# Token mixer's convolution: one PSUM bank for the turned spectra, two for the product back to time

## The reference

```python
logits = (x @ Wl.T + bl).reshape(Bq, Tq, H, K)          # K = 31 taps, H = 4 heads
w = softmax(where(valid, logits, -inf), axis=-1)
xg = x.reshape(Bq, Tq, H, d)[:, clip(pos, 0, Tq - 1)]
y = einsum('bthk,btkhd->bthd', w, xg).reshape(Bq, Tq, Cq)
y = y.transpose(0, 2, 1) + bias[None, :, None]
z = conv_general_dilated(y, Wc, (1,), 'VALID')           # Wc: 512 x 128 x 31
z = selu((z + bc[None, :, None]).transpose(0, 2, 1))
return z @ W2.T + b2                                     # 512 -> 128
```

## Time and profile before

| | before |
|---|---|
| median of 3 runs (lowest, highest) | 2428.52 us (2428.08, 2430.85) |
| profiled execution, its own time | 2426.93 us |
| its span | 2425.1 us |
| PE busy | 2096.5 us (86%) |
| DVE busy | 1616.2 us (67%) |
| ACT busy | 1200.1 us (49%) |
| POOL busy | 914.1 us (38%) |
| mean granted clock of TensorE | 0.932 |

### The profile page before, as it was taken

The page is one execution under the profiler, slowest core; times in us unless marked ns, Lnnn a source line. Parts: engine busy times, 40 slices in busy tenths (PEclk is TensorE's granted clock), DMA queues, the critical chain, the costliest instruction groups (busy, mean ns, idle before and its releaser), DMA issues. The chain is left out here.

```text
span 2425.1 us, 43279 instructions
## 1 busy us (share of the span) xinstructions
PE 2096.5 (86%) x14951; PEld 1497.0 (62%) x14951; DVE 1616.2 (67%) x3612; ACT 1200.1 (49%) x2015; POOL 914.1 (38%) x763
## 2 busy tenths in 40 slices
PE   6789999969997799999999997999999995687761
PEld 5568887835553566666666665777777773555540
DVE  5333456447775888888888874766766765666663
ACT  2333344335552567666767674655656552332330
POOL 0000000014443577777778781000000001876772
PEclk9899999979998799999999999999999996668995
DMA  7670000049900100000000000000000001214554
GB/s 271 228 259 26 26 28 10 1 189 419 396 5 1 70 1 1 0 0 0 0 0 0 0 1 20 1 0 0 0 0 0 0 1 46 89 42 129 169 144 156
DMA packets 64710, 165.38 MB, mean 68 GB/s; under 512 B 12450, under 2 KB 43476, under 8 KB 55100
## 3 DMA queue, kind: packets, MB, share of 16 engines
q1 hardware_dynamic: 51580, 148.24, 17.1%
q0 software_dynamic: 7104, 12.71, 1.5%
q10 hardware_dynamic: 5888, 2.62, 0.4%
HBM read 68.62 MB, written 96.86 MB: 68 GB/s over the span
## 5 line engine op out<-in xcount | busy, mean ns | idle before, releaser
L1279 POOL TENSOR_TENSOR c_both<-c_hid 128x512 f32<-128x512 f32 x384 | 492.0, 1289 | 142.4 <-ACT c_hid L1252 104.8
L1252 ACT ACTIVATE c_hid<-c_scaled,c_b 128x1024 f32<-128x1024 f32 x384 | 437.0, 1150 | 171.1 <-DVE c_scaled L1326 156.2
L1326 DVE TENSOR_TENSOR c_scaled<-c_p_h,c_shares 128x1024 f32<-128x1024 f32 x384 | 454.6, 1215 | 79.2 <-PE c_p_h L1195 77.9
L1200 PE MATMUL c_p_o<-c_both,c_w 128*128 128x512 f32 x768 | 390.7, 591 | 0.0
L1193 PE MATMUL c_p_h<-c_x_hi,c_w_hi 128*128 128x512 f32 x384 | 290.8, 757 | 2.6 <-DVE c_w_lo L1349 2.6
L642 POOL TENSOR_TENSOR d_ln_rstd<-d_ln_var,d_ln_power 128x2 f32<-128x2 f32 x48 | 33.5, 697 | 526.1 <-DVE d_ln_var L638 526.1
L1200 PEld LDWEIGHTS c_p_o<-c_both,c_w 128*128 128x128 f32 x768 | 144.4, 188 | 35.5 <-issue 2.2
L247 POOL COPY a_work<-a_vec 128x64 f32<-128x64 f32 x4 | 1.2, 303 | 409.1 <-PE a_p_A L338 223.6
L1510 PEld LDWEIGHTS d_p_s<-d_kk,d_q_bd 128*128 128x128 f32 x768 | 123.9, 192 | 45.9 <-issue 45.9
L1195 PE MATMUL c_p_h<-c_x_hi,c_w_lo 128*128 128x512 f32 x384 | 152.0, 396 | 0.0
L1194 PE MATMUL c_p_h<-c_x_lo,c_w_hi 128*128 128x512 f32 x384 | 151.8, 395 | 0.0
(11 more groups left out here) (327 smaller groups left out, 4591.5 us busy)
## 6 DMA issues: line engine op xcount, KB each, us to landing
slots<-b_blank SPq DMA_DIRECT2D x56, 1040.0 KB, 23.8
band_scratch<-a_work SPq DMA_DIRECT2D x16, 1024.0 KB, 5.3
a_work<-band_scratch SPq DMA_DIRECT2D x16, 1023.5 KB, 7.8
e_wb<-e_weights SPq DMA_DIRECT2D x63, 164.0 KB, 2.8
a_raw<-in_Wc SPq DMA_DIRECT2D x16, 512.0 KB, 3.7
e_xb<-slots SPq DMA_DIRECT2D x63, 130.0 KB, 2.2
e_yb<-e_again SPq DMA_DIRECT2D x12, 512.0 KB, 5.6
a_work<-in_x_tok SPq DMA_DIRECT2D x16, 256.0 KB, 7.4
```

The source lines that it names most:

```text
L1200: nc.tensor.matmul(p_o[s][:, 0:N], w2[:, q, :], both[q % SLOTS][:, :], start=(q == 0), stop=(q == NQ - 1)).then_inc(s_down, 1)
L1252: nc.scalar.activation(hid[q % SLOTS][:, :, :], scaled[q % SLOTS][:, :, :], ACT.Gelu, bias=b1[:, q:q + 1]).then_inc(s_ge, 1)
L1279: nc.gpsimd.tensor_tensor(both[q % SLOTS][:, :], hid[q % SLOTS][:, 0, :], hid[q % SLOTS][:, 1, :], ALU.add).then_inc(s_bo, 1)
L1326: v.tensor_tensor(scaled[q % SLOTS][:, :, :], p_h[q % SLOTS][:, 0:N].unsqueeze(1).to_broadcast([128, 2, N]), shares[s][:, :, :], ALU.mult) ...
```

## The change

`turn` writes only p_A[0], now also called p_turn, and waits for the copy of the turn just before. `to_time` writes p_A[1] and p_y by turns (p_conv is now a list of two) and waits for the `selu` two steps back instead of the one just before. `exp_z` and `selu` read the bank of their step. Because p_A[1] is used by the next dense part, `product` gets a wait at i = 1, for the `selu` of the last step that used it. No computing instruction is added or taken away, and no order of a stream is changed.

```diff
-        p_conv, p_out = p_y, p_log
+        p_turn, p_conv, p_out = p_A[0], [p_A[1], p_y], p_log
@@ product
+                if i == 1 and o > 0:
+                    pe.wait_ge(s_rz, NG * o - 1)
@@ turn
-                if g >= 2:
-                    pe.wait_ge(s_zt, k - 1)
+                if g >= 1:
+                    pe.wait_ge(s_zt, k)
                 for n in range(GB):
-                    last = nc.tensor.transpose(p_A[g % 2][0:NF2 + 1, n * 128:(n + 1) * 128], zs[:, g * GB + n, :],
+                    last = nc.tensor.transpose(p_turn[0:NF2 + 1, n * 128:(n + 1) * 128], zs[:, g * GB + n, :],
                                                ident[:, :])
@@ to_time
                 pe.wait_ge(s_zt, k + 1)
-                if k >= 1:
-                    pe.wait_ge(s_rz, k)
+                if k >= 2:
+                    pe.wait_ge(s_rz, k - 1)
                 for n in range(GB):
-                    last = nc.tensor.matmul(p_conv[:, n * SP:(n + 1) * SP], zt[g % 2][:, n, :], idft[:, :],
+                    last = nc.tensor.matmul(p_conv[g % 2][:, n * SP:(n + 1) * SP], zt[g % 2][:, n, :], idft[:, :],
@@ turned_out
-                nc.scalar.copy(zt[g % 2], p_A[g % 2][0:NF2 + 1, :].rearrange("j (n o) -> j n o", n=GB)).then_inc(s_zt, 1)
+                nc.scalar.copy(zt[g % 2], p_turn[0:NF2 + 1, :].rearrange("j (n o) -> j n o", n=GB)).then_inc(s_zt, 1)
@@ exp_z, and selu likewise
-                nc.scalar.activation(ez[g % 2], p_conv[:, 0:N].rearrange("o (n s) -> o n s", n=GB), ACT.Exp,
+                nc.scalar.activation(ez[g % 2], p_conv[g % 2][:, 0:N].rearrange("o (n s) -> o n s", n=GB), ACT.Exp,
```

More of the change, by code:

```diff
@@ L528, in selu @@
                 dve.wait_ge(s_ez, k + 1)
-                v.tensor_scalar(rz[g % 2], p_conv[:, 0:N].rearrange("o (n s) -> o n s", n=GB), -SELU_ALPHA,
+                v.tensor_scalar(rz[g % 2], p_conv[g % 2][:, 0:N].rearrange("o (n s) -> o n s", n=GB), -SELU_ALPHA,
                                 -SELU_ALPHA, ALU.add, ALU.max).then_inc(s_rz, 1)
```

## The result

The changed kernel takes 2426.78 us against 2430.7 us for the kernel before (medians of 20 runs each). The ratio is 0.9984, with a 95% interval of 0.9977 to 0.9990: 3.9 us less, between 2.4 and 5.6. That is a gain of 0.16%, just under the 0.2% that the prediction drew as its bound; the interval (0.10 to 0.23%) reaches past it. One of the 20 runs of the changed kernel was a slow one (3529 us at a granted clock of 0.554), and the ratio leaves it out.

The account below looks back on a forecast made before the run. Steps were taken to be closed by `to_time`'s one bank, with `project`'s wait for `add_h` nearly as late. -3.3 - 1.2 + 0.2 - 0.7 = -5.0 us gave a median near 2423.5, range 2420 to 2428.

Parts of the forecast that it names:

- The sum: Whole kernel: -3.3 - 1.2 + 0.2 - 0.7 = -5.0 us, median near 2423.5.
- Part 1, o = 3: Last product's time steps: two `to_time` banks give 2.285 us a step against 2.46, `project` then waiting for `add_h`; -3.3 us.
- Part 1, the pairs: Step pairs of o = 0 to 2: nothing gained, weights still every 5.9 us, since `project` still waits for `add_h`.
- The tails of o = 0 to 2: End of each of three products: the last `selu`s start earlier, 0.4 us each (0 to 0.7), -1.2 us.
- Part 2: One bank for turned spectra: hidden in steady steps; starts cost +0.2 us for three products, +0.39 in o = 3.
- Rival (c): Time steps: the turn waits for ACT, steps 2.77 us, pairs 0.95 longer; +28 us, 2456; chance 0.04.
- Part 3: Added wait in `product` (i = 1): cost 0, at most 0.12 us in each of three products.
- Part 4, the clock: Last `project` of o = 3: a shorter pause keeps the clock up, 0.9 against 1.62 us; -0.7 us (0 to -0.7).
- Rival (b): Last product held by a loop of equal length, only tails left: about -1.5 us, 2427; chance 0.16.
- Rival (a): Time steps: TensorE becomes the bound, 1.91 us a step in the last product; about -27 us, 2401; chance 0.05.
- Rival (d): Time steps: pauses from shuttling between banks lower the clock; +19 us in the last product alone, 2443; chance 0.04.

Follow-up runs that it names:

- out2_after: The changed kernel with a second bank for `project`'s result in o = 3 only; ratio to the kernel before 0.9969.
- mid_before: Kernel before with `project` one step later, a third z, and `add_h` of g - 3 between the two instructions of `selu` of g - 1; ratio 1.0005.
- turn_only: Kernel before with one bank for the turned spectra, `to_time` keeping its single bank; ratio to the kernel before 1.0002.
- x_after: Changed kernel with `project` one step later, a third z, and `add_h` of g - 3 ahead of `selu` of g - 1; ratio to the kernel before 0.9921.
- mid_after: Changed kernel with later `project`, third z, and `add_h` of g - 3 between the two instructions of `selu` of g - 1; ratio to the kernel before 0.9936.
- x2_after: As x_after, with `add_h` of step 14 ahead of DVE's first copy of the next dense part; ratio to the kernel before 0.9902, median 2404.94 us.
- lag_after: Changed kernel with `project` one step later, a third z, and `add_h` of g - 4 ahead of `selu` of g - 1; ratio to the kernel before 1.0049.
- conv_o3: Kernel before with a second bank for `to_time` in o = 3 only, the turns keeping two banks; ratio to the kernel before 0.9994.
- lag_before: Kernel before with `project` one step later, a third z, and `add_h` of g - 4 ahead of `selu` of g - 1; ratio 1.0090.
- after_again: The changed kernel once more, beside lag_before and lag_after on the same chip; ratio to the kernel before 0.9982.

## Why the prediction was right, point by point

- **The sum.** -5.0 was forecast, the trace shows -4.8 in the convolution, and the 20 runs -3.9 (-2.4 to -5.6). The sign, the place and the smallness were right. That the total came so close is partly luck: the -0.7 of the clock did not come, and the tails gave 0.6 more than the sum had; the two nearly cancel. The median forecast, 2423.5, is 3.3 below the 2426.78 measured; 2.2 of these are the kernel before, which had 2428.52 in three runs and 2430.7 in twenty. The chances stood at 0.44 for faster and 0.48 for the same; the measured 0.16% falls in the latter.
- **Part 1, o = 3: right.** -3.3 was forecast for the last `selu`; it starts 39.99 after the stage's first turn in before and 36.73 in after, -3.26. The alternating steps came at 1.98 and 2.62 (1.91 and 2.66 forecast): the link from `project` to the next `to_time` is 1.08, and `to_time` to `project` 0.90, where 1.05 and 0.86 stood. That `project` waits for `add_h` was shown by out2_after.
- **Part 1, the pairs: right.** 5.96 and 5.90 in both kernels. The loop through `add_h` and `project` (5.96) is longer than the one through `to_time`'s bank, which mid_before shows by itself: 5.73. Opening the shorter one gives nothing.
- **The tails of o = 0 to 2: undersized.** To o = 3 the change took 1.59 us off, where -1.2 + 0.2 = -1.0 stood. Each product lost 0.51 to 0.54. With the start's +0.1 (turn_only: 0.11 for three) the tails gave about 0.6 each and not 0.4. In o = 0 half of it lies ahead of the next dense part (from the last weights to its first load 7.30, before 7.57) and half in it, where the idle time before the last `project` has gone (from there to the first turn 29.71, before 29.96).
- **Part 2: right.** Starts cost +0.1 in all for three products (0.2 forecast) and 0.36 in o = 3 (0.39). In steady steps of after no turn waits for its copy. Rival (c) did not occur, even in x_after, where TensorE moves fastest.
- **Part 3: right.** The first load of the product that now waits (i = 1) starts 0.43 after the last `project` in both kernels (266.56 and 266.99 in after, 267.57 and 268.00 in before).
- **Part 4, the clock: wrong.** The 0.7 us for the last `project` did not come: it took 1.62 in after too, behind a pause of only 0.74:

```profile
483.22 0.88 PE L359 MATMUL a_p_log<-a_work,a_w 128*128 128x384 f32 x2 [0.87 <-DVE hT L547]
...
484.85 1.62 PE L359 MATMUL a_p_log<-a_work,a_w 128*128 128x384 f32 x2 [0.74 <-DVE hT L547]
486.50 0.56 DVE L547 SCALAR_TENSOR_TENSOR hT<-a_p_log,hT 128x384 f32<-128x384 f32 x1 [1.80 <-PE a_p_log L359]
```

  The failed step is that from the shorter pause to the full clock. The pause did shrink, from 1.57 to 0.74, but turn_only had before's 1.57 and kept the full clock, and the changed kernel took 1.62 in one execution and 1.36 in another. The length of the pause does not decide it. The runs point to a draw of the execution, which belongs in the range and not in the sum; neither of the two kernels itself was seen with 0.88, so for them that is not shown. Without it and with the tails at their true size the sum is -3.3 - 1.6 = -4.9, and the trace shows -4.8.
- **Rival (b)** is out by the trace (o = 3 gave its 3.2), and its -1.5 lies outside the interval of the runs (-2.4 to -5.6).
- **Rival (a) and the rule beside it.** The Trainium skill (Perfetto Trace Analysis, Optimization Strategy) says that a gap which repeats can mean too little SBUF or PSUM for the next tile. In o = 3 the traces agree: steps went from 2.46 to 2.30 with the second bank of `to_time`, and to 2.04 with a second one for p_out. In the pairs the gap stayed with the new bank (5.96); there p_out had no free bank, and what took the gap away was an earlier `add_h` with a third z. So the wait that the view names first need not be the buffer that is short.
- **Rival (d)**: the granted clock was 1.00 in the time steps of after, until 484.8, at the end of o = 3. The idle ahead of `project` had no effect on it.

## What to carry to other kernels

When a wait is to be removed, look in the order of time for the other loops that run through the same engine and compare their lengths; the gain is the difference, not the idle time listed under the wait. Here it was 2.46 against 2.30 us a step in o = 3, and 5.73 against 5.96 (nothing) in the pairs. Of two coupled loops one alone gives little: the second bank alone gave 4.8 us, the new order alone a loss of 1.9 (mid_before), both together 17.1 (mid_after), and with the end of the products mended too 23.8 (x2_after). The loss of mid_before comes from those ends; without their 4.6 us of idle time it would be a gain of 2.6, an estimate from its trace. In all three runs with the new order 0.7 of the difference is the last `project` at the full clock. An instruction moved earlier on a strictly ordered queue must be looked at for what it is now behind: `add_h` behind a copy that waits for this step's products cost more than the whole change gained (lag_after 281.27, after 268.37).

## What was not expected of the hardware

The last matmuls before the end of the phase ran at either level of the granted clock with equal pauses ahead: 0.88 us with pauses of 1.57 (turn_only) and 0.74 (conv_o3, mid_after, x_after), 1.62 us with pauses of 1.57 (before) and 0.74 (after, lag_before). Of the thirteen profiled executions four show the lower clock there (1.36 to 1.62). The clock also fell at different distances from the work: about 1.1 us after it had ended in before, 0.7 in after (granted clock 0.92 over 484 to 485 us and 0.50 from there), 1.8 in conv_o3 (0.58 over 491 to 492, after the last `project` had ended at 489.32). No rule for it was found in the order of work.

The runs of lag_before, lag_after and after_again stood beside runs of the kernel before of 2492.9 us and not 2430. The convolution took the same there (268.15 in after_again, 268.37 in after), and in the window from 1900 to 2000 us TensorE was busy for 95.92 us in both; the 60 us lie behind 2000 us, in the last mixture of experts, outside the change. Their cause is open; only ratios to the kernel before of the same runs are used.
